# A gather of graph edges on TensorE: the order of a tile's places, and where it waits for landed chunks

## What is computed

```python
agg = segment_sum(x[src], dst, num_segments=6250)      # both layers begin so
# layer 0
h = (1.0 + eps) * x + agg
h = relu(batch_norm(h @ W1 + b1, g1, be1))             # 512 -> 1024
h = relu(batch_norm(h @ W2 + b2, g2, be2))             # 1024 -> 512
x = layernorm(x + (x + h))
# layer 1
h = where(indeg[:, None] > 0, agg, x)
h = batch_norm(relu(h @ W.T + b), gamma, beta)         # 512 -> 512
x = layernorm(x + h)
```

## Time and profile before

| what | us |
|---|---|
| median of 3 runs (2880.34 to 2883.93) | 2883.85 |
| the profiled execution | 2885.93 |
| its span | 2884.2 |
| 23 pairs of the first gather | 94 to 1190 |
| 23 pairs of the second gather | 1637 to 2695 |

### The profile page before, as it was taken

One profiled execution on the slowest core, in us unless ns is written; L12 is line 12 of the kernel. 1 busy time (PEld: TensorE's weight loads), 2 busy tenths in 40 slices (PEclk: granted clock), 3 DMA queues, 4 the chain that ended last, 5 costly groups with the idle time before them and its releaser, 6 DMA issues. The chain is left out here.

```text
span 2884.2 us, 36034 instructions
## 1 busy us (share of the span) xinstructions
PE 2346.4 (81%) x8463; PEld 1505.5 (52%) x8464; DVE 1534.5 (53%) x2580; ACT 841.9 (29%) x1475; POOL 1585.6 (55%) x1731
## 2 busy tenths in 40 slices
PE   3888887888888888899996588887887979877885
PEld 2555554555555555578886344444444535444454
DVE  5455545454545454643337656554555646454658
ACT  2232323232323222355555312111121112121226
POOL 7666666666666666300002566666666666666633
PEclk9999898989999999999998699999998999998996
DMA  7676676666676766433326766666666666666668
GB/s 249 202 211 200 203 213 191 208 198 208 206 213 200 211 198 208 141 115 99 96 74 191 239 192 187 189 193 187 194 184 186 193 184 195 187 192 188 187 181 270
DMA packets 165529, 545.44 MB, mean 189 GB/s; under 512 B 28980, under 2 KB 32907, under 8 KB 160723
## 3 DMA queue, kind: packets, MB, share of 16 engines
q0 software_dynamic: 125120, 410.09, 49.2%
q1 hardware_dynamic: 17608, 78.33, 9.0%
q10 hardware_dynamic: 22744, 56.47, 5.7%
HBM read 493.18 MB, written 51.60 MB: 189 GB/s over the span
## 5 line engine op out<-in xcount | busy, mean ns | idle before, releaser
L880 PE MATMUL psum<-ring,select 128*125 x2400 | 1242.5, 620 | 22.6 <-issue 22.3
L592 POOL DMA_INDIRECT ring<-x_in,src_t x782 | 771.6, 987 | 421.0 <-issue 217.6
L592 POOL DMA_INDIRECT ring<-x_d,src_t x782 | 754.6, 965 | 406.6 <-issue 217.4
L923 PE MATMUL psum<-sumsT,w_hi 128*128 128x500 f32 x1248 | 695.4, 573 | 101.5 <-DVE h3T L725 38.6
L863 PE MATMUL psum<-rows_hi,select_r 128*125 128x512 f32 x600 | 369.6, 616 | 270.7 <-DVE rows_lo L694 151.5
L880 PEld LDWEIGHTS psum<-ring,select 128*125 128x125 f32 x2400 | 425.4, 196 | 221.8 <-issue 170.7
L694 DVE TENSOR_TENSOR rows_lo<-ring,rows_hi 128x512 fp32r<-128x512 f32 x605 | 390.5, 688 | 111.0 <-ACT rows_hi L1000 56.0
L1000 ACT ACTIVATE rows_hi<-ring 128x512 fp32r x605 | 346.5, 621 | 268.4 <-issue 208.0
L923 PEld LDWEIGHTS psum<-sumsT,w_hi 128*128 128x128 f32 x1248 | 245.9, 197 | 284.4 <-issue 175.3
L923 PE MATMUL psum<-sumsT,w_lo 128*128 128x250 f32 x1248 | 355.6, 285 | 6.0 <-issue 6.0
L863 PEld LDWEIGHTS psum<-rows_hi,select_r 128*125 128x125 f32 x600 | 120.3, 200 | 412.5 <-issue 224.4
(11 more groups left out here) (190 smaller groups left out, 2338.1 us busy)
## 6 DMA issues: line engine op xcount, KB each, us to landing
hidden_d<-of_layer ACTq DMA_DIRECT2D x50, 500.0 KB
act_f<-hidden_d SPq DMA_DIRECT2D x24, 1000.0 KB
ring<-x_in,src_t POOLq DMA_INDIRECT x782
ring<-x_d,src_t POOLq DMA_INDIRECT x782
sums<-x_in ACTq DMA_DIRECT2D x50, 250.0 KB
sums<-x_d ACTq DMA_DIRECT2D x50, 250.0 KB
rows_r<-x_in SPq DMA_DIRECT2D x6, 1120.0 KB
x_d<-rows_r SPq DMA_DIRECT2D x6, 1120.0 KB
```

The lines of the kernel that those rows point to most:

```text
L592: nc.gpsimd.indirect_dma_start(slot(c % S), None, table, bass.IndirectOffsetOnAxis(ap=index_of(c), axis=0)).then_inc(gathered[c % S], 16)
L880: whole = nc.tensor.matmul(agg(h), select[h][:, WHOLE_AT.index(p), :], of_chunk(pe, first, place), start=False, stop=n + 1 == WINDOW, skip ...
L923: last = nc.tensor.matmul(out, w[:, k, o * P:(o + 1) * P], moving, start=part == 0, stop=part >= len(parts) - 2, skip_group_check=True)
```

## The change

The places of a tile are put in another order: 0, 2, 1, 4, 3, 6, 5, ... and then the rest. The k-th split place stands at position 2k + 2 in place of 2k, and the whole places among them stand up to two positions earlier. Each whole place with an even index among the whole ones (0, 4, 8, 12, 16 in layer 0) waits for its own chunk and that of the next whole place. A slot counts as free one place later (`need` is raised by one). `EARLY` in layer 0 is 4 in place of 3: the fourth split place of the following pair is made at the end of an iteration by ScalarE (behind the first `store`, ahead of the read of product 5) and by VectorE (ahead of the add of product 7), and no more at the head of the next.

```diff
@@ order
-        order = []
-        for p in self.split_places(layer):
-            order += [p, p - 1]
-        return order + list(range(len(order), self.WINDOW))
+        split = self.split_places(layer)
+        whole = [p for p in range(self.WINDOW) if p not in split]
+        order = whole[:1]
+        for k, p in enumerate(whole[1:]):
+            order += [p] + split[k:k + 1]
+        return order
@@ need
-        nc.gpsimd.iota(self.need_all[:], [[2 * z.WINDOW, z.ALL_GROUPS], [1, z.STRIDE]], base=z.WINDOW + 1,
+        nc.gpsimd.iota(self.need_all[:], [[2 * z.WINDOW, z.ALL_GROUPS], [1, z.STRIDE]], base=z.WINDOW + 2,
-            link(nc.vector.scalar_tensor_tensor(self.need[:, a:b], m.bank(4 + n)[0:1, 0:b - a], 1.0 - z.WINDOW,
+            link(nc.vector.scalar_tensor_tensor(self.need[:, a:b], m.bank(4 + n)[0:1, 0:b - a], 2.0 - z.WINDOW,
@@ gather_phase
-    EARLY = 3 if layer == 0 else 2
+    EARLY = 4 if layer == 0 else 2
@@ vector
-                            low_rows(use[2], following, 1, EARLY)
+                            low_rows(use[2], following, 1, 3)
                             add_product(count, pair, 6)
                             statistics(count, after, pair, 5, 6)
+                            low_rows(use[2], following, 3, EARLY)
                             add_product(count, pair, 7)
@@ tensor
-                            if p > SPLIT_AT[-1] and (n % 2 == 0 or layer == 0):
-                                later = p if layer == 0 else p + 1
+                            if WHOLE_AT.index(p) % 2 == 0:
+                                later = WHOLE_AT[WHOLE_AT.index(p) + 1]
                                 pe.wait_ge(landed, begin + (last_place if later + 1 == WINDOW else later))
@@ scalar
-                            high_rows(following_begin, use[2], following, 2, EARLY)
+                            high_rows(following_begin, use[2], following, 2, 3)
                             read_product(stored, after, pair, 4)
                             store(after, pair, 0)
+                            high_rows(following_begin, use[2], following, 3, EARLY)
```

## The result

| | us |
|---|---|
| before, median of 17 runs (2872.70 to 2899.06) | 2885.33 |
| changed, median of 17 runs (2857.15 to 2882.46) | 2865.18 |
| ratio, with its 95% interval | 0.9937 (0.9921 to 0.9952) |
| span of the profiled execution | 2860.1 (before 2884.2) |

The change gains 18 to 20 us; the forecast was 51. The direction and the first moves inside the trace are as predicted, and most of the gain isn't there. The granted clock over the span is 0.915, from 0.910.

The account below looks back on a forecast made before the run. It took TensorE, waiting for VectorE's late rows_lo, as what bounds the kernel, not GpSimd. Terms 29.6 + 30 + 13 = 73 us, less 15.5 and 6.5, gave 51: 2883.85 - 51 = 2833, stated as 2834, range 2795 to 2883.

Parts of the forecast that it names:

- What a stall is worth: Stall time taken off TensorE in both gathers was counted as kernel time: 73 us in sum, 51 after deductions.
- Holds move or end at their own times: Doubt whether ScalarE's holds, ending when they did, lose TensorE's gain: 15.5 and 6.5 us were taken off the 73.
- second kind: First gather, TensorE's stall at the fourth split place: making it an iteration earlier saves 2.5 us in 12 pairs, 30 us.
- First kind: First gather, TensorE's stall at the seventh split place: the new order saves 1.97 us in 15 pairs, 29.6 us.
- Second gather: TensorE's stall at the third split place there: some 9 pairs gain 1.5 us each, 13 us.
- the sign of a mistake: TensorE's waits for landed chunks (L883) over 30 us in the changed trace would show the prediction wrong.
- Landed waits and slots: Both gathers: added waits for landed chunks and slots freed one place later were taken to cost 0 each.
- The slower rival: Slots freed later in the second gather's ring of 20 lengthen GpSimd's waits by 107 us: 2931; slower 0.13, mostly this.
- The page's rule on branches: ScalarE's hold follows a fetch after its branch back and moves ahead with it; the sum would keep its 22 us.
- Absorbed: Rival: ScalarE's holds end at their own times, TensorE waits longer at the product piece or turn: 2884; chance 0.10.
- The clock's price: Both gathers: 183 us counted as half-speed time following the stalls; an eighth of it back gives 2788.
- holds move: Rival: ScalarE's holds are tied to its own branch, so nothing is lost: 2811, or 2788 with clock; chance 0.14.

Follow-up runs that it names:

- e1_early4: The kernel before with only the fourth split place made early (EARLY 4 in layer 0); ratio 1.0007 to the kernel before.
- e4_layer1: The changed order and waits in layer 1 alone, layer 0 as before, slots freed later in both; ratio 1.0001 to the kernel before.
- g2_lesspe_before: The kernel before with the product of each split place's rows_lo cut from 512 to 32 columns; ratio 0.9990 to the kernel before.
- g1 runs: The kernel before and the changed one, each with every second gather left out after the ring's first filling; ratios 0.8183 and 0.8139 to the kernel before.
- g1_fewer_before: The kernel before with every second gather left out once the ring has been filled; ratio 0.8183 to the kernel before.
- e2_early3: The changed kernel with EARLY back at 3 in layer 0; ratio 0.9940 to the kernel before.
- e3_layer0: The changed order, waits and EARLY in layer 0 alone, layer 1 with the old order and waits, slots freed later in both; ratio 0.9950 to the kernel before.
- i1_one_behind: The changed kernel with layer 0's places in natural order, the k-th split place at position 2k + 1; ratio 0.9943 to the kernel before.
- e6_waits: The kernel before with the changed kernel's waits for landed chunks, in its own order; ratio 1.0008 to the kernel before.
- e5_need: The kernel before with slots freed one place later in both layers; ratio 0.9981 to the kernel before.

## Why the prediction was right in direction and too large

**What a stall is worth (failed, and it is the step that decided).** The sum took stall time off TensorE, 29.6 + 30 + 13 us, and handed it to the end at full or half value. The runs give 0 for the 30 (e1_early4), 0 for the 13 (e4_layer1), and 14 to 18 us for layer 0's order, whose stall was put at 29.6. The value rested on "GpSimd is busy 707.8 us of the 1096 ...; it isn't the bound." The 0.30 us between gathers that follow each other belong to them; with 198.1 us of these, GpSimd was taken 905.9 of the 1096 us, as much as TensorE with 915.7. g2_lesspe_before shows that TensorE's time has little value here, and the g1 runs that it has some once half of the gathers are gone.

**Holds move or end at their own times (the doubt was right, its size wrong).** I took 22 us off for stalls that would only move. e1_early4 shows that all 30 of the second kind do. The timelines suggest how. This is the longest stall of the changed kernel's first gather; TensorE, then ScalarE, then VectorE, then GpSimd:

```profile
657.07 1.02 PE L883 MATMUL psum<-ring,select 128*125 x2
667.20 0.78 PE L926 MATMUL psum<-sumsT,w_hi 128*128 128x500 f32 x1 [9.10 <-DVE sumsT L719]
```

```profile
650.10 1.15 ACT L1003 ACTIVATE rows_hi<-ring 128x512 fp32r x2 [2.20 <-issue]
665.19 0.59 ACT L993 ACTIVATE sumsT<-psum 128x500 fp32r<-128x500 f32 x1 [13.94 <-remote]
```

```profile
665.88 1.26 DVE L719 TENSOR_TENSOR sumsT<-psum,sumsT 128x500 fp32r<-128x500 f32 x2 [12.90 <-ACT sumsT L993]
```

```profile
660.35 0.95 POOL L594 DMA_INDIRECT ring<-x_in,src_t  x1 [0.30 <-issue]
661.60 0.95 POOL L594 DMA_INDIRECT ring<-x_in,src_t  x1 [0.30 <-issue]
665.76 0.94 POOL L594 DMA_INDIRECT ring<-x_in,src_t  x1 [3.22 <-remote]
```

ScalarE stands from 651.3 to 665.19, while GpSimd issues gather behind gather. GpSimd runs out of free slots at 662.55 and pauses, and ScalarE comes back 3.59 us after that run's last gather had begun. The earlier trace rows is the same picture: ScalarE came back at 573.91, and the last gather of GpSimd's run had begun at 570.74, 3.17 before (rows above). I counted all of ScalarE's idle stretches of over 5 us in both gathers, whatever they waited for: in the trace of before 49 of 98 end 2 to 4 us after the start of the last gather of a run; ends spread evenly would give some 11. In e1_early4 it is 53 of 99, in the changed kernel 47 of 97. Not all are so: the hold of the earlier trace rows ended in the middle of a run.

So about half of the holds last until GpSimd pauses, and GpSimd would pause when TensorE, stalled behind the held ScalarE, frees no more slots. This is argued from times in the traces, with the fewer gathers of g1_fewer_before (runs of 2.6 gathers in place of 11.7, and in the first gather no idle stretch of ScalarE over 5 us) as the one experiment that bears on it; a kernel in which GpSimd pauses of its own accord wasn't run. What in the chip ties ScalarE to GpSimd's gathers stays open. It would explain why the gain is absorbed: two more places that TensorE makes ahead of a stall free two more slots, and GpSimd runs 2 x 1.25 us longer before it pauses.

**First kind (29.6 us; the moves inside the trace right, the mechanism of the gain not borne out).** The stalls at the seventh split place did go, L866 has 7.6 us, and others came at the product pieces, as said: 76.6 us there, against "up to some 70", and 45 at the turn, against 30. TensorE's waits fell by 27 us in all, and GpSimd's waits for slots by 18 (203.4 to 185.4 us). That the latter is the gain of the medians is an observation of one execution each; e2_early3 and e3_layer0 say by their times that 14 to 17 us go with layer 0's order. But i1_one_behind has the same gain with 60.1 us of this stall still there. That the forecast had the direction right is in part luck: the stalls that were to give 60 of the 73 us aren't shown to give any of it.

**Second kind (30 us): failed.** 0 by e1_early4, and none by e2_early3 within the changed order. The reading was thin too: "I count 12 of these", but TensorE waited in front of the fourth split place in every pair, and over 1 us in 14 of 23.

**Second gather (13 us): failed.** 0 by e4_layer1. The waits went from L866 to L883, which I had named as the sign of a mistake (over 30 us). It is 54.1, and yet the time didn't rise (1.0001). TensorE's waits lie elsewhere, and the time is the same, as with e1_early4.

**Landed waits and slots (0 each): right** within 0.4%, by e6_waits and e5_need. The slower rival (the ring of the second gather) is out: GpSimd's slot waits there went from 189.2 to 181.7 us.

**The page's rule on branches.** The Trainium skill, page "Runtime: NRT & Kernel Launch", section "Instruction fetch mechanics", would have tied the hold to ScalarE's branch back. With four of five branches back of the loop over pairs gone the time was 1.0022 and the stalls were there. So the rule isn't refuted, but a hold here doesn't need this branch.

**Absorbed (0.10)** was the rival that came nearest to the truth: it holds for the second kind and for the second gather.

**The clock's price** in the rival "holds move" is misnamed: a granted clock of 0.91 over 1096 us is 188 us at the lower level (half speed), and the 99 us are what they cost.

## What to carry to other kernels

Add to an engine's busy time the "issue" gaps inside its runs of equal instructions before you rule it out as the bound (here 707.8 us became 905.9 of 1096). Before costing stalls one by one, take work off the stalled engine in one run, and look at the granted clock of that run: if the time doesn't move, moving stalls is worth little too. When the trace moved as you said, run a variant that keeps the stall you removed: here it was as fast.

## What was not expected of the hardware

A gather of 128 rows by GpSimd took 0.95 us in most cases and 0.30 more before the next started; with 64 rows the mean was 0.93 (0.98 with 128), so it is mostly the instruction that costs, not the rows. While such gathers followed each other, ScalarE stood for up to 14 us with its inputs there, and in about half of these cases went on 2 to 4 us after the last gather of a run had begun. With half of the gathers the kernel took 0.8183 of its time.
